# A selective scan's loads: C rows in a ring of 20, diagonal weights in three half pieces, x^T in three half blocks, B ahead from a small table

## The reference, cut to what matters

```python
def step(h, inp):
    x_t, dt_t, B_t, C_t = inp
    dA = jnp.exp(A[None] * dt_t[..., None])
    dB = (1.0 - dA) / (A[None] + 1e-08) * B_t[:, None, :]
    h = jnp.clip(dA * h + dB * x_t[..., None], -10.0, 10.0)
    y_t = jnp.sum(C_t[:, None, :] * h, -1) + D_param * x_t
    return (h, y_t)
```

## Time and profile before

| | |
|---|---|
| three runs | 4684.94 us median (4679.14 to 4690.98) |
| the profiled execution | 4684.51 us, span 4682.7 us |
| scan stage | first scan at 1165.26 us, last product begun at 3710.4 us |
| PE, DVE, ACT, POOL busy over the span | 91%, 79%, 68%, 70% |
| granted TensorE clock | 0.966 mean |

### The profile page before, as it was taken

How to read it: one execution, slowest core, us unless ns; L and a number is a source line. 1 busy time by engine, 2 the same in 40 slices (tenths; PEclk the granted TensorE clock), 3 DMA queues, 4 the chain that set the end, 5 groups by cost and what they waited for, 6 DMA issues and landing times. The chain is left out here.

```text
span 4682.7 us, 48765 instructions
## 1 busy us (share of the span) xinstructions
PE 4279.3 (91%) x14186; PEld 2517.8 (54%) x14186; DVE 3716.3 (79%) x4288; ACT 3178.3 (68%) x5820; POOL 3285.3 (70%) x1676
## 2 busy tenths in 40 slices
PE   2999999995999999999999999999999759999999
PEld 1777777773444444444444444444444337777777
DVE  5888888884999999999999999999999744444443
ACT  1655666654999999999999999999999611211111
POOL 0233323222889999999999999999999757777772
PEclk9999999997999999999999999999999879999999
DMA  5565556665566556656655665566556444545550
GB/s 182 188 201 184 199 184 195 195 201 183 150 185 172 155 161 185 169 156 167 187 161 149 174 187 160 151 182 188 159 152 184 135 150 153 161 154 164 168 158 31
DMA packets 591700, 786.65 MB, mean 168 GB/s; under 512 B 129712, under 2 KB 332848, under 8 KB 573512
## 3 DMA queue, kind: packets, MB, share of 16 engines
q1 hardware_dynamic: 580872, 762.56, 54.6%
q10 hardware_dynamic: 10560, 20.97, 1.2%
HBM read 540.17 MB, written 245.18 MB: 168 GB/s over the span
## 5 line engine op out<-in xcount | busy, mean ns | idle before, releaser
L1091 DVE TENSOR_TENSOR_SCAN g<-dd,carry,ps_a 128x512 f32<-128x512 f32 x2048 | 2408.9, 1272 | 157.2 <-ACT dd L964 122.9
L953 POOL TENSOR_TENSOR q<-g,cc 128x1024 f32<-128x1024 f32 x1024 | 2379.6, 2385 | 205.7 <-DMA cc<-c_d 125.1
L1031 PE MATMUL ps_y<-q,w_s 128*128 128x512 f32 x4096 | 2210.5, 622 | 128.0 <-POOL q L953 127.3
L1020 PE MATMUL ps_d<-dm,xk 99*128 99x512 f32 x2048 | 1570.1, 768 | 49.0 <-DMA dm<-band_d 39.8
L975 ACT ACTIVATE ps_a<-dt_s,small 128x512 f32<-128x512 f32 x2048 | 1475.7, 721 | 5.4 <-DVE g L1091 5.4
L964 ACT ACTIVATE dd<-ps_d 128x512 f32<-128x512 f32 x2048 | 1265.9, 619 | 197.4 <-PE ps_d L1020 185.2
L1031 PEld LDWEIGHTS ps_y<-q,w_s 128*128 128x128 f32 x4096 | 719.8, 193 | 847.1 <-POOL q L953 503.4
L1020 PEld LDWEIGHTS ps_d<-dm,xk 99*128 99x128 f32 x2048 | 393.7, 193 | 653.8 <-issue 412.9
L517 PE MATMUL ps_r_f<-xnt_hi,w_hi 128*128 128x512 f32 x1024 | 431.8, 422 | 13.8 <-DVE w_lo L683 13.8
L354 POOL TENSOR_TENSOR xnt_lo<-xnt_f,xnt_hi 128x512 fp32r<-128x512 f32 x64 | 85.2, 1331 | 478.8 <-ACT xnt_hi L392 478.8
L517 PE MATMUL ps_r_f<-xnt_lo,w_hi 128*128 128x512 f32 x1024 | 410.1, 400 | 0.0
(11 more groups left out here) (160 smaller groups left out, 4407.5 us busy)
## 6 DMA issues: line engine op xcount, KB each, us to landing
w_s<-w_d SPq DMA_DIRECT2D x128, 1024.0 KB, 5.2
xk<-xt_d SPq DMA_DIRECT2D x768, 132.0 KB
xt_d<-xt_f SPq DMA_DIRECT2D x256, 256.0 KB, 3.1
cc<-c_d SPq DMA_DIRECT2D x128, 512.0 KB, 11.5
dm<-band_d SPq DMA_DIRECT2D x192, 264.0 KB
xs_d<-xs_f SPq DMA_DIRECT2D x128, 256.0 KB, 2.7
zs_d<-zs_f SPq DMA_DIRECT2D x128, 256.0 KB, 2.6
dt_d<-lg_f SPq DMA_DIRECT2D x32, 1024.0 KB, 4.4
```

Of the source, the lines that this page charges most:

```text
L953: pool.tensor_tensor(q[:, s % QB:s % QB + 2, :], g[:, s % GB:s % GB + 2, :], cc[:, n:n + 2, :], ALU.mult).then_inc(s_q, 2)
L1020: pe.matmul(ps_d[:, i % 2, :], xk[:, (2 * blk + i // HALF) % XB, i % HALF, :], dm[:, i, :, :].rearrange("p t n -> p (t n)"), start=True, s ...
L1031: pe.matmul(ps_y[:, blk % 2, :], w[:, blk % 2, n * P:(n + 1) * P], q[:, s % QB, :], start=(n == 0), stop=(n == NS - 1)).then_inc(s_n, 1)
L1091: dve.tensor_tensor_scan(g[:, s % GB, :], dd[:, m % 2, n, :], ps_a[:, s % AB, :], carry[:, m, n:n + 1], ALU.add, ALU.mult).then_inc(s_g, 1)
```

## The change

Five edits, all in how data gets to the scan:

1. C rows lie in a ring of 10 pairs (20 rows). Pairs 0 and 1 of the next chunk are asked for in blocks 3 and 4, pairs 2 to 7 in block 7, each after POOL has multiplied with the pair whose place it takes.
2. The diagonal weight is loaded in halves of 512 KB into three places, where two whole ones lay before. The first half is asked for where the whole was, the second at the end of SP's block.
3. x^T has three half-block places, not four, and is asked for half a block later.
4. `b_ahead` comes from a table `ba_d` of 64-byte rows that two small DRAM-to-DRAM gathers fill when the scan starts; SP waits for them.
5. In `front` some semaphores are merged; the same work is waited for.

```diff
-    XB, DTB, CN = 4, 3, 2
+    XB, DTB, CN, WB, CR = 3, 3, 2, 3, 10
...
-        w = sb("w_s", [P, 2, NS * P], c=c)
+        w = sb("w_s", [P, WB, NS * P // 2], c=c)
...
-        cc = sb("cc", [P, NS, CH], c=c)
+        cc = sb("cc", [P, CN * CR, CH], c=c)
...
-                def load_w(blk):
+                def load_w(blk, h):
                     if blk < BLOCKS:
-                        sp.dma_start(w[:, blk % 2, :], w_d[blk % MD, :, W_DIAG:W_DIAG + NS * P]).then_inc(s_wl[blk % 2], 16)
+                        slot = (2 * blk + h) % WB
+                        sp.dma_start(w[:, slot, :], w_d[blk % MD, :, bass.ds(W_DIAG + NS * P // 2 * h, NS * P // 2)])\
+                            .then_inc(s_wl[slot], 16)
 
                 def load_c(ch, i):
                     if ch < CHUNKS:
-                        if ch > 0:
-                            sp.wait_ge(s_q, multiplied(STEPS * ch - NS + CN * (i + 1)))
+                        pair = ch * (NS // CN) + i
+                        slot, old = pair % CR, pair - CR
+                        if old >= 0:
+                            sp.wait_ge(s_q, multiplied(STEPS * (old // (NS // CN) + 1) - NS + CN * (old % (NS // CN) + 1)))
...
                 def load_ahead(ch):
-                    b, k = ch // NCH, ch % NCH
-                    row = xp_d[b, 1:1 + NS, bass.ds(k * CH, 1)].rearrange("n o -> (n o)")
-                    sp.dma_start(b_ahead[:, :], row.partition_broadcast(P),
+                    sp.dma_start(b_ahead[:, :], ba_d[ch // NCH, ch % NCH, :].partition_broadcast(P)).then_inc(s_ba, 16)
+
+                def gather_ahead(b):
+
+                    sp.dma_start(ba_d[b, :, :], xp_d[b, 1:1 + NS, 0:LEN].rearrange("n (k t) -> k n t", t=CH)[:, :, 0],
                                  allow_slow_non_contiguous=True).then_inc(s_ba, 16)
...
                 load_x(1, 0)
+                sp.wait_ge(s_dps, HALF)
                 load_x(1, 1)
-                load_w(0)
+                load_w(0, 0)
+                load_w(0, 1)
                 load_c(0, 2)
                 load_c(0, 3)
+                for b in range(BATCH):
+                    gather_ahead(b)
+                sp.wait_ge(s_ba, 16 * BATCH)
                 load_ahead(0)
                 load_prev(0)
-                sp.wait_ge(s_dps, HALF)
-                load_x(2, 0)
                 for blk in range(BLOCKS):
...
                     sp.wait_ge(s_dps, made)
-                    load_x(blk + 2, 1)
+                    load_x(blk + 2, 0)
                     sp.wait_ge(s_a, NS * blk + 1)
                     load_dt(blk + 2)
                     load_prev(blk + 1)
                     if m == 0:
-                        for i in range(4 if ch == 0 else 6, 8):
+                        for i in range(4 if ch == 0 else 8, 8):
                             load_c(ch, i)
...
+                    if m in (3, 4):
+                        load_c(ch + 1, m - 3)
                     if m == MD - 1:
-                        load_c(ch + 1, 0)
+                        load_c(ch + 1, 2)
                     if blk > 0:
                         sp.wait_ge(s_n, NS * blk)
-                    load_w(blk + 1)
+                    load_w(blk + 1, 0)
...
                     if m == MD - 1:
-                        load_c(ch + 1, 1)
-                        load_c(ch + 1, 2)
+                        load_c(ch + 1, 3)
+                        load_c(ch + 1, 4)
                     if blk + 1 < BLOCKS:
                         sp.wait_ge(s_dps, made + HALF)
                     if m == MD - 2 and more:
                         load_b(ch + 1, 1)
-                    load_x(blk + 3, 0)
+                    load_x(blk + 2, 1)
                     if m == MD - 1 and more:
-                        load_c(ch + 1, 3)
+                        load_c(ch + 1, 5)
                         load_ahead(ch + 1)
...
                     if m == MD - 1:
-                        load_c(ch + 1, 4)
-                        load_c(ch + 1, 5)
+                        load_c(ch + 1, 6)
+                        load_c(ch + 1, 7)
+                    if blk + 1 < BLOCKS:
+                        sp.wait_ge(s_n, NS * blk + NS // 2)
+                    load_w(blk + 1, 1)
...
             @block.tensor
...
-                        pe.wait_ge(s_wl[blk % 2], 16 * (blk // 2) + 16)
+                    half, at = 2 * blk + n // (NS // 2), n % (NS // 2) * P
+                    if n % (NS // 2) == 0:
+                        pe.wait_ge(s_wl[half % WB], 16 * (half // WB) + 16)
```

More of the change, by code:

```diff
@@ L62, in build @@
         y_d = nc.dram_tensor("y_d", [BATCH, MD, P, LEN], F32).ap()
+        ba_d = nc.dram_tensor("ba_d", [BATCH, NCH, NS], F32).ap()
         ident = sb("ident", [P, P])
@@ L73, in build @@
             front(nc, sb, sem, t_in, ident, ones, minus_half, margin, within, clips, xs_d, dt_d, zs_d, xp_d, xt_d, bt_d, c_d)
-        scan(nc, sb, sem, ident, clips, xs_d, dt_d, xp_d, xt_d, bt_d, band_d, c_d, w_d, y_d)
+        scan(nc, sb, sem, ident, clips, xs_d, dt_d, xp_d, xt_d, bt_d, band_d, c_d, w_d, y_d, ba_d)
         ffn(nc, sb, sem, t_in, ident, minus_half, xs_d, zs_d, xp_d, w_d, y_d, out)
@@ L217, in front @@
         s_wt, s_x, s_one, s_hi, s_lo, s_b1 = S("weights"), S("x"), S("one"), S("hi"), S("lo"), S("b1")
-        s_wd, s_wdl, s_wdo = S("wd"), S("wdl"), S("wdo")
         s_st, s_pow, s_xn, s_tr, s_te, s_xl = S("stats"), S("pow"), S("xn"), S("tr"), S("te"), S("xl")
@@ L302, in _ @@
                     sp.dma_start(dst, src).then_inc(s_wt, 16)
-                sp.wait_ge(s_wdl, 1)
-                sp.dma_start(w_dt[2 * NX:NX3, :].bitcast(F32), low_dt.bitcast(F32)).then_inc(s_wdo, 16)
+                sp.wait_ge(s_lo, 3)
+                sp.dma_start(w_dt[2 * NX:NX3, :].bitcast(F32), low_dt.bitcast(F32)).then_inc(s_wt, 16)
                 load_x(1)
@@ L445, in _ @@
                                    stage[:, :, :].rearrange("p m t -> p (m t)"), ACT.Copy).then_inc(s_hi, 1)
-                act.activation(w_dt[:, :], raw_dt, ACT.Copy).then_inc(s_wd, 1)
+                act.activation(w_dt[:, :], raw_dt, ACT.Copy).then_inc(s_hi, 1)
                 for ch in range(CHUNKS):
@@ L458, in _ @@
                     else:
-                        act.wait_ge(s_wdl, 1)
+                        act.wait_ge(s_lo, 3)
                     keep_z(ch, 3)
@@ L581, in _ @@
                     if ch == 0:
-                        pe.wait_ge(s_wdo, 16)
+                        pe.wait_ge(s_wt, 14 * 16)
                     for i in range(SUB):
@@ L686, in _ @@
                                       ALU.subtract).then_inc(s_lo, 1)
-                dve.wait_ge(s_wd, 1)
-                dve.tensor_tensor(low_dt, raw_dt[0:NX, :], w_dt[0:NX, :].bitcast(F32), ALU.subtract).then_inc(s_wdl, 1)
+                dve.wait_ge(s_hi, 3)
+                dve.tensor_tensor(low_dt, raw_dt[0:NX, :], w_dt[0:NX, :].bitcast(F32), ALU.subtract).then_inc(s_lo, 1)
                 dve.wait_ge(s_b1, 1)
                 dve.wait_ge(s_lo, 2)
-                dve.wait_ge(s_wdo, 16)
+                dve.wait_ge(s_wt, 14 * 16)
                 for ch in range(CHUNKS):
@@ L747, in _, with scan @@
                 dve.wait_ge(s_fl, 3)
-def scan(nc, sb, sem, ident, clips, xs_d, dt_d, xp_d, xt_d, bt_d, band_d, c_d, w_d, y_d):
+def scan(nc, sb, sem, ident, clips, xs_d, dt_d, xp_d, xt_d, bt_d, band_d, c_d, w_d, y_d, ba_d):
     STEPS = MD * NS
@@ L785, in scan @@
         s_dm = [S(f"dm{i}") for i in range(PIECES)]
-        s_xk, s_cc = [S(f"xk{i}") for i in range(XB)], [S(f"cc{i}") for i in range(NS // CN)]
+        s_xk, s_cc = [S(f"xk{i}") for i in range(XB)], [S(f"cc{i}") for i in range(CR)]
         s_dtl = [S(f"dt{i}") for i in range(DTB)]
-        s_wl, s_xp, s_yo = ([S(f"{n}{e}") for e in range(2)] for n in ("w", "xp", "yo"))
+        s_xp, s_yo = ([S(f"{n}{e}") for e in range(2)] for n in ("xp", "yo"))
+        s_wl = [S(f"w{i}") for i in range(WB)]
         s_dps, s_dd = S("dps"), S("dd")
@@ L939, in _ @@
                     sp.wait_ge(s_xp[e], 16 * BLOCKS // 2)
-                sp.wait_ge(s_ba, 16 * CHUNKS)
+                sp.wait_ge(s_ba, 16 * (BATCH + CHUNKS))
             @block.gpsimd
@@ L947, in _ @@
                     ch, n = s // STEPS, s % NS
+                    pair = ch * (NS // CN) + n // CN
                     if s % STEPS < NS:
-                        pool.wait_ge(s_cc[n // CN], ch * 16 + 16)
+                        pool.wait_ge(s_cc[pair % CR], 16 * (pair // CR) + 16)
+                    rows = cc[:, CN * (pair % CR):CN * (pair % CR) + CN, :]
                     pool.wait_ge(s_g, s + 2)
@@ L952, in _ @@
                         pool.wait_ge(s_n, s - QB + 2)
-                    pool.tensor_tensor(q[:, s % QB:s % QB + 2, :], g[:, s % GB:s % GB + 2, :], cc[:, n:n + 2, :],
+                    pool.tensor_tensor(q[:, s % QB:s % QB + 2, :], g[:, s % GB:s % GB + 2, :], rows,
                                        ALU.mult).then_inc(s_q, 2)
@@ L1028, in sum_state @@
```

(8 more changed lines are left out.)

4 lines of the change are left out of this document (2 added, 2 removed).

## The result

The changed kernel takes 4556.44 us (median of 4 runs, 4553.38 to 4556.73) against 4685.11 us before: a ratio of 0.9724, with an interval from 0.9707 to 0.9741. The forecast was 4557. The profiled execution took 4556.5 us with a span of 4554.7, so 128.0 us of span are to be accounted for.

The account below looks back on a forecast made before the run. The prediction took late C transfers, stopping POOL and DVE at chunk boundaries, as the bound, with DVE next. From 4684.5 us it took 127.6 (134.8 + 8.6 - 8.3 - 7.5), giving 4557; range 4539 to 4612.

Parts of the forecast that it names:

- The sum: Scan stage: DVE's idle 134.8 plus 8.6 for slow scans, less 8.3 and 7.5 kept, gives 127.6 us gained.
- the scans' 8.6 us: DVE's scans that run slow just after a stop: 2408.9 - 2400.3 = 8.6 us to be gained.
- The start: First block of the scan: of DVE's 10.3 us of stops 8.3 stay, bounds 4 and 13.
- late x^T: Chunk boundary: a half lands 1.1 us late, charged 0.5 us at each of 15 boundaries, 7.5 us, bounds 0 and 45.
- w's second half: SP's queue at the boundary: it lands within 0.5 us of when PE wants it; nothing charged.
- my own signs of being wrong: Wrong if DVE's idle per boundary exceeds 3 us, its scan exceeds 1.172 us, or w's second half holds PE.
- b_ahead: Boundary queue: 128 elements for 2048 save 5.5 us of queue, between 2 and 6.2.
- The hold of SP: SP held 7.58 us on the y store behind b_ahead; the hold goes, but alone doesn't price b_ahead.
- The stop did not move to x^T and w's second half: First rival: at the boundary x^T or w's second half is late by 3 to 7 us, 4617 us; chance 0.17.
- A half piece of w does not cost a whole one: Second rival: a half piece costs as much queue as a whole, 4.5 us; 4692 us, no gain; chance 0.04.
- Three places of x^T alone: Third rival: three places are too few in every block; 4857 us at 2.5 us of lateness; chance 0.03.

Follow-up runs that it names:

- the two runs with less work in one engine: Changed kernel with POOL multiplying 256 of the 512 columns: 4553.04 us; changed kernel with DVE's scan over 480 of 512 columns: 4533.05 us.
- the run with x^T alone: Kernel before with x^T in three half places only, w whole: 4686.37 us, ratio 1.0005.
- The run with the new start: Changed kernel with ACT issuing the gathers, SP not waiting for them before its loop, and C pairs 4 to 7 asked for earlier: 4544.56 us.
- the run without the table: Changed kernel with the old b_ahead load of 2048 words, without the gathers and SP's wait for them: 4657.18 us, ratio 0.9938.
- the runs with one kind each: Kernel before with x^T in three half places only: 4686.37 us; kernel before with w in half pieces only: 4702.36 us.
- another order: Changed kernel with the old b_ahead load and no gathers, w's second half asked for ahead of C pairs 6 and 7: 4658.99 us.

## Why the prediction was right

**What bounds.** The late C pair was the cause of the stops, and with it gone DVE is the bound. POOL's wait for cc went from 125.1 to 14.3 us, all of it in the first block (12.0 and 2.2). DVE's 2048 scans take 2400.3 us, and the two runs with less work in one engine confirm it from both sides: less for POOL changes nothing, less for DVE gives just POOL's pace.

**The sum, term by term.** Of DVE's idle time in the stage 18.1 us are left (39.9 less the 21.76 before its first scan), where the sum left 8.3 + 7.5 = 15.8; the scans' 8.6 us came out exactly (2408.9 to 2400.3). That makes 134.8 - 18.1 + 8.6 = 125.3. The first scan also begins 1.9 us earlier (1163.38 against 1165.26), which is in no term, and 0.8 us lie behind the last scan: 128.0. The 1.9 us are put on none of the edits: with the old front stage the run with x^T alone began at 1162.28, and the runs' first scans lie between 1161.5 and 1166.4.

**The start was sized wrongly.** The sum kept 8.3 us there and 13.4 stayed (0.62, 0.55, 12.28). The sum let the gathers land soon behind pair 3; SP waited 12.3 us for them. The run with the new start, in which C no longer stands behind this wait, has 2.8 us of stops. The prediction also counted two halves of x^T ahead of C pairs 4 to 7; the code has three, and four before. No term rests on that.

**The boundary was sized a little too high.** 7.5 us were charged for late x^T, and 4.1 were lost at the boundaries. It was charged as 0.5 us at each of 15, and came as 1.0 and 3.0 us at two. The item was right to be at the edge and only half right in its name: in the changed kernel PE waits 6.2 us for x^T behind the start and 9.2 for w. I had said of w's second half that it lands within 0.5 us of its use and had charged nothing; in the run without the table it is the one waited for. By the letter one of my own signs of being wrong came up, that w's second half holds PE, at 2.0 us at most. The two errors of the sum, 5 us too little at the start and 3 too much here, nearly cancel. That the forecast lies within 1 us of the median is better than its working.

**b_ahead** was credited with 5.5 us of queue, between 2 and 6.2. The bytes moved show 4.3 us at the boundary above, inside these bounds and a little under the credit. Without the table the kernel is 101 us slower, 6.7 us for each of 15 boundaries, which is more than the queue time of the load. One thing that adds to it is PE's clock: in that run it was 0.50 from 1344 to 1352 us, around the end of the 7.97 us stop, and a product of d took 1.42 us. How the 101 us divide was not measured. The hold of SP gave the sign and not the size, as stated.

**The rivals.** The stop did not move to x^T and w's second half, but it is near: take the table away and it does, at about 6.7 us a boundary. A half piece of w does not cost a whole one: 512 transfers of 256 KB in place of 256 of 512 KB take 4560.69 against 4556.44 us, less than the interval of either ratio. The Trainium skill, page "DMA: Bandwidth & Descriptors", section "Measured (HBM→SBUF, 128 partitions, SWDGE, issued from GpSimd)", asks for transfers of at least 1 MiB, for DMAs issued from GpSimd. For SP's queue in this kernel it is not borne out, by the same two times (4560.69 and 4556.44 us). Three places of x^T alone are 4686 against 4683: nothing in any block, as the calm landings of the earlier trace rows had said.

**What was wrong in the expectations behind it.** I took the pieces for free while C's stop covers them. They cost 21 us, and the runs with one kind each put that on w's second half. The lead in steps, 16 for both halves, said nothing of the place in the queue: at a boundary that half stands behind ten more transfers than the whole had. The order of these was left open by the sum, which only counted the x^T half behind it.

## What to carry to other kernels

When an engine stops at the same spot in every outer loop, follow the late transfer to the queue that asked for it and count what stands ahead of it there; a small load of thousands of single words can be among the largest items, and the bytes moved in the windows behind it show its price. Give each transfer a due time and a landing time from the trace, and ask which comes last once the first is cured: here this gave the size of the next stop within some 2 us, and only half its name. Where everything at the boundary is due, another order gained nothing here (4658.99 against 4657.18 us); less in the queue, and asking in the calm part, did. Do not let the queue's issuer wait for a small transfer before it asks for large ones.

## What was not expected of the hardware

- The load of 8 KB as 2048 single words took 4.3 us of the queue, what 1.0 MB takes at the 234 GB/s of the earlier trace rows, and the DMA engines were only 0.42 busy meanwhile. As 128 rows of 64 bytes it doesn't show: 238 GB/s at the same place.
- Two gathers of 128 words each, DRAM to DRAM, kept SP waiting 12.3 us, the last 6 us of it beside DMA engines that were 0.01 busy.
- Splitting 512 KB transfers in two cost 4.25 us for 256 added ones, and some 0.14 us for each of those at the boundaries (an estimate from DVE's 8.3 us of added stops over 60).
- DVE's scan of 512 columns took 1.172 us whether POOL was multiplying all the time or half of it.
